# Attention and split convolution on one core: alternating the two kinds of attention blocks, and dividing by the row sums at the copy-out

## Chip, cores and metric

One core of a Trainium2 chip. The metric is the device time of one execution in microseconds. TensorE (PE) multiplies, VectorE (DVE) and ScalarE (ACT) work on tiles, GpSimd (POOL) too, and SyncE (SP) issues the DMAs.

## What is computed

Input x is 4 images of 256 channels and 64 x 64 pixels. The two layers, cut to what matters:

```python
# layer 0: attention over the 4096 pixels of an image
q, k, v = Wq @ xf, Wk @ xf, Wv @ xf                 # 32, 32 and 256 rows
attn = softmax((q.T @ k) / sqrt(32), axis=-1)       # 4096 x 4096
x = gamma * (Wo @ (v @ attn.T)) + x
# layer 1: in patches of 8 x 8
low = mean over 2 x 2;  high = p - upsample(low)
low = prelu(bn(mag_w @ low + mag_b))
high = prelu(bn(phase_w @ concat(high, roll(high, 1 row)) + phase_b))[:256]
out = upsample(low) + high
```

## The kernel before

**Tiling.** The queries of an image are worked on in 8 chunks of 512, so there are 32 chunks g. Values and output projection are one matrix, u. Each 32-bit number that needs it is a sum of two shorter ones (ph and pl, uh and ul), so a block is weighed with three products. The keys of an image are 32 tiles of 128. They come in two kinds, in 32 units t of a chunk:

- 16 *scored tiles* "d": TensorE multiplies keys with queries (`scores`, line 584, two tiles ahead), ScalarE takes two exponentials (`probabilities`, 754), VectorE forms the low part pl (`low_probabilities`, 1045), TensorE weighs: 12 matmuls into the four output banks O0 to O3 (`weigh_tile`, 621). Column 256 of uh is 1, so the sum of each row comes out as column C of the bank.
- 16 *kept blocks* "k": their scores were computed for the maxima one chunk earlier and kept in `saved` with queries on the partitions. ScalarE takes two exponentials (`slot_probabilities`, 763, at unit EXP_AT), VectorE the low part (`slot_low_probabilities`, 1049, at unit LOW_AT), SyncE transposes by DMA into a ring of four (`turn_slot`, 367), TensorE weighs 12 matmuls into one bank, k % 4 (`weigh_slot`, 636).

**Order.** It is written out by hand. UNITS (lines 53 to 56) is d0 to d5, then k0 d6 k1 d7 and so on to k9 d15, then k10 to k15. EXP_AT is 5 units ahead of a block's weighing, LOW_AT 3 (4 for the last ones). In between stand the other tasks of a chunk (lines 86 to 108), which use two banks M in turn: keys, queries and u of the next image ("kq", "u"; t = 0, 2), the output turned back ("y"; 5, 6), the two convolutions ("low" 20, 21; "high" 22, 24), 32 matmuls for the maxima of the next queries ("max", t = 3 to 28), and "negmax" (t = 30) with the queries' shift.

**Plans.** FULL is the plan of the first 24 chunks, LAST of the next 7, FINAL of the last: in the last image nothing is projected for a next one (no kq, u), and first scores are issued one unit before the chunk's end.

**The head of a chunk.** `copy_out` (748 on ScalarE for banks 0 and 2, 1028 on VectorE for 1 and 3) copies 257 columns of a bank when the last block of that bank, k12 to k15, is weighed. `normalise` (1033) on VectorE then takes the reciprocal of the sums, multiplies by the image's gain and scales the four copies. The first `weigh_tile` of the next chunk waits for the copies, the y tasks for `normalise`.

**SyncE's program of a FULL chunk**, each line waiting for its inputs, and everything behind it waiting too:

```python
sp.dma_start(xb, ...)                                   # 397
sp.wait_ge(qsave_ready, NCH + g + 1)                    # 398, the kq task, t = 0
sp.dma_start(flat(q_dram), qsave[96:128, :])            # 399
turn_slot(g, 0)
sp.wait_ge(qst_ready, g + 2); fetch_q(...)              # 403 to 406, low_q at t = 1
turn_slot(g, 1)
emptied(("u", 1)); store uh; store ul                   # 409 to 411, t = 2
sp.wait_ge(out_ready, g + 1); store z                   # 412 to 414
turn_slot(g, 2); turn_slot(g, 3); load xr; turn_slot(g, 4) ...
```

In LAST chunks lines 397 to 399 and 409 to 411 are left out, in FINAL 403 to 406 too. At an image's last chunk (`ends_image`) the loads of the next image's u stand between the `turn_slot` calls.

**The head of an image.** `find_scale` (903) on VectorE reduces the bound of x, GpSimd reduces it over the partitions (`reduce_bound`, 1187), and VectorE makes the scale of u from it. It runs in `before_image` (1134), ahead of the image's first chunk, and ScalarE waits for its result (`scaled`, line 842) ahead of that chunk.

Of the kernel before, what the change touches and what calls it, by code (L numbers as in the profile page):

```python
# [113 lines left out]
def attention_conv(nc, x, wqk, wv, wo, phase_w, mag_w, params, gamma, alpha, out, q_dram):  # L114
# [7 lines left out]
    with ctx:  # L122
# [27 lines left out]
        spare = sb("spare", [128, 10])  # L150
# [25 lines left out]
        oraw = sb("oraw", [128, SUB, UW])  # L176
# [26 lines left out]
        O = [ctx.enter_context(nc.psum_tensor(f"O{i}", [128, 512], f32)) for i in range(SUB)]  # L203
# [28 lines left out]
        u_direct_loaded, u_turned_loaded = sem("u_direct_loaded"), sem("u_turned_loaded")  # L232
        o02_out, o13_out, rs_step, on_ready = sem("o02_out"), sem("o13_out"), sem("rs_step"), sem("on_ready")
# [22 lines left out]
        def turns(eng, turn, before_image=None, before_last=None, image_end=None):  # L256


            inner = NCH - 1 if image_end else NCH
            with eng.Fori(0, B // 2 - 1) as pair_i:  # L260
                for parity in range(2):
                    if before_image:
                        before_image(pair_i * 2 + parity, parity)
                    with eng.Fori(0, inner) as c:
# [6 lines left out]
            with eng.Fori(0, inner) as c:  # L271
# [54 lines left out]
        def _(sp):  # L326
# [48 lines left out]
            def load_u(m, filled):  # L375

                sp.dma_start(uh_flat[:, m * SUB * UW:(m + 1) * SUB * UW], uh_dram[m]).then_inc(filled, 16)
                sp.dma_start(ul_flat[:, m * SUB * C:(m + 1) * SUB * C], ul_dram[m]).then_inc(filled, 16)

            def load_direct_u(g, m):  # L380

                sp.wait_ge(d_weighed, ND * g + SUB * (m + 1))
                load_u(m, u_direct_loaded)

            def load_turned_u(g, m):

                sp.wait_ge(k_weighed, NK * g + slot_of(SUB - 1, m) + 1 + RING)
                load_u(m, u_turned_loaded)

            def turn(g, parity, c, plan, scans, ends_image=False):  # L390
# [37 lines left out]
                turn_slot(g, 4)  # L428
                if ends_image:
                    load_direct_u(g, 1)  # L430
                turn_slot(g, 5)
# [4 lines left out]
                turn_slot(g, 8)  # L436
                if ends_image:
                    load_direct_u(g, 2)
                turn_slot(g, 9)
# [9 lines left out]
                if ends_image:  # L449
                    load_direct_u(g, 3)  # L450
                turn_slot(g, 14)
                turn_slot(g, 15)
                if ends_image:
                    load_turned_u(g, TURNED[2])
# [14 lines left out]
            sp.wait_ge(u_direct_loaded, 16 + 128 * (B - 1))  # L469
            sp.wait_ge(u_turned_loaded, 16 + 128 * (B - 1))  # L470
# [6 lines left out]
        def _(pe):  # L477
# [115 lines left out]
            def tasks(g, plan, keys_next, t):  # L593
                for n, task in plan.numbered.get(t, []):
# [6 lines left out]
                    elif kind == "y":  # L601
                        pe.wait_ge(on_ready, g + 2)
# [18 lines left out]
            def weigh_tile(g, i):  # L621

                if i == 0:
                    pe.wait_ge(u_direct_loaded, 128 * (g // NCH) + 16)
                pe.wait_ge(lo_ready, ND * g + i + 1)

                for j in range(SUB):
# [5 lines left out]
                    ins = nc.tensor.matmul(O[j][:, 0:UW], pl[:, i % 4, q], uh[:, i, :], start=False, stop=False)  # L633
# [47 lines left out]
            for n, task in TAIL.numbered[0]:  # L681
                pe.wait_ge(m_free[n % 2], use(TAIL, ALL, n))
                if task[0] == "y":
                    pe.wait_ge(on_ready, ALL + 2)
# [10 lines left out]
        def _(act):  # L695
# [52 lines left out]
            def copy_out(g, j):  # L748

                act.wait_ge(k_weighed, NK * g + RING - SUB + j + 1)  # L750
                act.wait_ge(high_ready, g + 1)
                nc.scalar.activation(oraw[:, j, :], O[j][:, 0:UW], ACT.Copy).then_inc(o02_out, 1)

            def probabilities(g, i):
                act.wait_ge(s_filled, ND * g + i + 1)
                if i >= 4:
                    act.wait_ge(d_weighed, ND * g + i - 3)
# [14 lines left out]
            def take(bank, task, g, parity, c):  # L772
# [6 lines left out]
                elif kind == "u":  # L779
                    act.wait_ge(u_stored, 32 * g + 32)  # L780
# [22 lines left out]
            def turn(g, parity, c, plan, scans):  # L803

                if plan is FULL:
# [52 lines left out]
        def _(dve):  # L858
# [10 lines left out]
            nc.vector.memset(half[:, :, :], -0.5).then_inc(on_ready, 1)  # L869
# [4 lines left out]
            nc.vector.memset(spare[:, 2:3], 0.0).then_inc(proj_free, 4)  # L874
            nc.vector.memset(spare[:, 3:4], 0.0).then_inc(k_weighed, RING)
            for i in range(RING):
                nc.vector.memset(spare[:, 6 + i:7 + i], 0.0).then_inc(turned[i], 16)
            nc.vector.memset(spare[:, 5:6], 0.0).then_inc(u_direct_loaded, 16)
            nc.vector.memset(spare[:, 4:5], 0.0).then_inc(u_turned_loaded, 16)
# [41 lines left out]
            dve.wait_ge(scanned0, NCH)  # L921
            find_scale(0, 0)
# [104 lines left out]

# [239 lines left out]
```

## Time and profile before

| | us |
|---|---|
| runs of the kernel before, median (lowest to highest) | 2342.92 (2342.83 to 2344.77) |
| the profiled execution, its own time | 2340.45 |
| its span | 2338.5 |
| TensorE busy, matmuls | 2205.9 (94%) |
| VectorE busy | 1782.4 (76%) |
| ScalarE busy | 1431.6 (61%) |
| GpSimd busy | 677.7 (29%) |
| mean granted clock of TensorE | 0.984 |

Busy times of matmuls have modelled ends, so TensorE's share isn't its share of peak. "Granted clock" is the part of the full 2.4 GHz that TensorE was given. A timeline row says what an instruction waited for in brackets: the idle time of its engine before it, and who released it. "SPq" is the queue in which SyncE issues. A line in the rows is a line of the kernel before.

### The profile page before, as it was taken

The numbers are of one execution on the slowest core, as the hardware profiler recorded it, in microseconds if no ns is written. First come the engines' busy times: TensorE is split into PE (matmuls) and PEld (weight loads), VectorE is DVE, ScalarE is ACT, GpSimd is POOL, SyncE is SP. The second block draws the span as 40 slices with busy tenths as digits, with TensorE's granted clock in tenths as the row PEclk, the third lists the DMA queues.
The fourth block names the chain that finished last, engine by engine and source line by source line (L and its number), as shares of the span: only waits on it lengthen the run. The fifth ranks groups of instructions, "written<-read, shape, count | busy, mean of one in ns | idle before, by whom it ended". The sixth has DMA issues, their size and how long they took to land.

```text
span 2338.5 us, 48099 instructions
## 1 busy us (share of the span) xinstructions
PE 2205.9 (94%) x16373; PEld 1764.1 (75%) x16373; DVE 1782.4 (76%) x3388; ACT 1431.6 (61%) x2547; POOL 677.7 (29%) x891
## 2 busy tenths in 40 slices
PE   5799999999989999999998999999999999999997
PEld 4577777777767777777777777777777777777776
DVE  6777877777867788877786877777877777778764
ACT  3457666657656666666656666566665656666663
POOL 3232332232322323322232321323322232233321
PEclk8799999999999999999999999999999999999998
DMA  4254444454554444444474443443445444344443
GB/s 159 59 115 94 99 109 102 84 117 99 135 131 85 110 107 92 109 108 97 93 168 102 99 99 72 104 96 91 103 111 133 75 89 93 77 82 88 84 86 64
DMA packets 596617, 235.02 MB, mean 101 GB/s; under 512 B 547072, under 2 KB 548352, under 8 KB 596576
## 3 DMA queue, kind: packets, MB, share of 16 engines
q1 hardware_dynamic: 596576, 234.51, 45.5%
q8 instruction: 22, 0.36, 0.1%
q14 instruction: 19, 0.16, 0.0%
HBM read 67.67 MB, written 32.53 MB: 43 GB/s over the span
## 4 chain that ended last, share of the span: by engine, by line
PE 64%; DVE 15%; issue 10%; DMA 5%; ACT 3%; POOL 1%; SPq 1%; DVEq 0%; ACTq 0%; POOLq 0%
PE M L482 13%; PE M L519 7%; PE O L631 7%; PE O L633 6%; PE O L632 6%; PE O L644 6%; PE O L646 6%; PE O L645 6%; DVE pq L1052 5%; DMA pt<-pq 4%; PE S L590 4%; DVE saved L947 4%; DVE pmax L943 2%; DVE pl L1047 2%; PE M L500 1%
## 5 line engine op out<-in xcount | busy, mean ns | idle before, releaser
L758 ACT ACTIVATE ph<-S 128x512 f16<-128x512 f32 x512 | 307.6, 601 | 525.5 <-PE S L590 524.8
L644 PE MATMUL O<-uh,pt 128*128 128x257 f16 x2048 | 568.2, 277 | 16.9 <-DMA pt<-pq 16.7
L631 PE MATMUL O<-uh,ph 128*128 128x257 f16 x2048 | 570.3, 278 | 4.5 <-DVE pl L1047 4.1
L633 PE MATMUL O<-uh,pl 128*128 128x257 f16 x2048 | 563.2, 275 | 0.0
L632 PE MATMUL O<-ul,ph 128*128 128x256 f16 x2048 | 561.8, 274 | 0.0
L646 PE MATMUL O<-uh,pt 128*128 128x257 f16 x2048 | 559.0, 273 | 0.0
L645 PE MATMUL O<-ul,pt 128*128 128x256 f16 x2048 | 555.7, 271 | 0.0
L947 DVE TENSOR_SCALAR_CACHE_REDUCE saved<-M 128x512 f32<-128x512 f32 x512 | 344.0, 687 | 257.0 <-PE M L519 253.0
L1047 DVE TENSOR_TENSOR pl<-p,ph 128x512 f16<-128x512 f32 x512 | 402.6, 787 | 60.5 <-ACT p L761 59.1
L519 PE MATMUL M<-kst,qst 96*128 (+1 forms) x1024 | 424.0, 442 | 20.9 <-DVE saved L947 16.2
L1052 DVE TENSOR_TENSOR pq<-saved,pq 128x512 f16<-128x512 f32 x512 | 387.6, 757 | 19.2 <-ACT saved L770 19.1
L943 DVE TENSOR_REDUCE pmax<-M 128x1 f32<-128x512 f32 (+1 forms) x512 | 341.4, 684 | 70.8 <-PE M L519 67.8
L769 ACT ACTIVATE pq<-saved,nbias 128x512 f16<-128x512 f32 x512 | 369.2, 721 | 1.3 <-DMA pt<-pq 1.3
L770 ACT ACTIVATE saved<-saved,nbias 128x512 f32<-128x512 f32 x512 | 367.9, 719 | 0.0
L761 ACT ACTIVATE p<-S 128x512 f32<-128x512 f32 x512 | 307.7, 601 | 0.0
L631 PEld LDWEIGHTS O<-uh,ph 128*128 128x128 f16 x2048 | 201.1, 98 | 133.7 <-issue 92.6
L644 PEld LDWEIGHTS O<-uh,pt 128*128 128x128 f16 x2048 | 198.8, 97 | 121.1 <-issue 52.4
L1215 POOL TENSOR_TENSOR zlow<-zlow,zlneg 128x256 f32<-128x256 f32 x32 | 23.8, 744 | 797.5 <-DVE zneg L1067 797.5
L590 PE MATMUL S<-qcur,kst 128*128 128x512 f32 x512 | 238.1, 475 | 16.5 <-ACT p L761 14.1
L519 PEld LDWEIGHTS M<-kst,qst 96*128 96x128 f32 x1024 | 188.3, 191 | 60.8 <-DVE saved L947 27.1
L633 PEld LDWEIGHTS O<-uh,pl 128*128 128x128 f16 x2048 | 201.7, 98 | 26.1
L646 PEld LDWEIGHTS O<-uh,pt 128*128 128x128 f16 x2048 | 197.8, 97 | 29.2
(161 smaller groups left out, 2907.4 us busy)
## 6 DMA issues: line engine op xcount, KB each, us to landing
xr<-in_x SPq DMA_DIRECT2D x53, 512.0 KB, 3.8
out_y<-z SPq DMA_DIRECT2D x33, 512.0 KB, 3.0
xb<-in_x SPq DMA_DIRECT2D x25, 512.0 KB, 3.7
pt<-pq SPq DMA_TRANSPOSE x512, 3.1
qraw<-q_scratch SPq DMA_DIRECT2D x99, 64.0 KB, 2.0
uh_scratch<-uh_next SPq DMA_DIRECT2D x24, 257.0 KB, 3.2
uh<-uh_scratch SPq DMA_DIRECT2D x24, 257.0 KB, 3.2
ul_scratch<-ul_next SPq DMA_DIRECT2D x24, 256.0 KB, 3.1
```

The source lines that it names most:

```text
L519: return nc.tensor.matmul(bank[:, :], qst[0:96, j * 128:(j + 1) * 128], kst[0:96, keys_at], start=True, stop=True)
L631: nc.tensor.matmul(O[j][:, 0:UW], ph[:, i % 4, q], uh[:, i, :], start=(i == 0), stop=False)
L632: nc.tensor.matmul(O[j][:, 0:C], ph[:, i % 4, q], ul[:, i, :], start=False, stop=False)
L633: ins = nc.tensor.matmul(O[j][:, 0:UW], pl[:, i % 4, q], uh[:, i, :], start=False, stop=False)
L644: nc.tensor.matmul(O[j][:, 0:UW], pt[:, k % RING, i, :], uh[:, t, :], start=False, stop=False)
L645: nc.tensor.matmul(O[j][:, 0:C], pt[:, k % RING, i, :], ul[:, t, :], start=False, stop=False)
L646: ins = nc.tensor.matmul(O[j][:, 0:UW], pt[:, k % RING, SUB + i, :], uh[:, t, :], start=False, stop=(ends and i == SUB - 1))
L769: nc.scalar.activation(pq[:, k % RING, 0, :], saved[:, k, :], ACT.Exp, scale=SCALE, bias=bias)
L943: nc.vector.tensor_reduce(pmax[:, j, ds(m, 1)], bank[:, :], AX.X, ALU.max).then_inc(free, 1)
L947: nc.vector.tensor_scalar(saved[:, slot_of(j, m), :], bank[:, :], 0.0, None, ALU.add, ALU.max, accum_out=pmax[:, j, m:m + 1]).then_inc(fre ...
L1047: nc.vector.tensor_tensor(pl[:, i % 4, :], p32[:, i % 2, :], ph[:, i % 4, :], ALU.subtract).then_inc(lo_ready, 1)
L1052: nc.vector.tensor_tensor(pq[:, k % RING, 1, :], saved[:, k, :], pq[:, k % RING, 0, :], ALU.subtract).then_inc(slot_low, 1)
```

## The change

Units now alternate from the first to the last: d0 k0 d1 k1 ... d15 k15. Exponentials of block k run at unit 2k - 4 (blocks 0 and 1 ahead of the chunk's own work), low parts at 2k - 2, at most 27. The four output banks are one tensor, O_all. Only k15 ends the chunk, so all banks are read after it: VectorE takes the reciprocal of the four sums from the banks themselves (`find_gains`), and both copies are made with that factor; `normalise` is gone. ScalarE's and VectorE's copies now wait for the gains. u has a semaphore for each eighth, and its loads move in SyncE's program. The scale is found inside the image's first chunk, after unit 0's low part, and ScalarE waits for it only at its first u task. Lines 397 to 415 of SyncE's program are as they were, apart from the u load taken out behind block 2.

```diff
-RISE = 6
-UNITS = [("d", i) for i in range(RISE)]
-for i in range(ND - RISE):
-    UNITS += [("k", i), ("d", RISE + i)]
-UNITS += [("k", k) for k in range(ND - RISE, NK)]
-AT = {unit: t for t, unit in enumerate(UNITS)}
-EXP_AT = [AT["k", k] - 5 for k in range(NK)]
-LOW_AT = [AT["k", k] - (3 if k < ND - RISE else 4) for k in range(NK)]
+UNITS = [unit for i in range(ND) for unit in (("d", i), ("k", i))]
+EXP_AT = [2 * k - 4 for k in range(NK)]
+LOW_AT = [min(2 * k - 2, MT - 5) for k in range(NK)]
...
             def load_direct_u(g, m):
 
-                sp.wait_ge(d_weighed, ND * g + SUB * (m + 1))
-                load_u(m, u_direct_loaded)
+                sp.wait_ge(d_weighed, ND * g + ND + SUB * (m + 1))
+                load_u(m)
...
                 turn_slot(g, 2)
-                if ends_image:
-                    sp.wait_ge(u_stored, 32 * g + 64)
-                    sp.sem_inc(turn_seen, 1)
-                    load_direct_u(g, 0)
                 turn_slot(g, 3)
...
             def weigh_slot(g, k):
 
-                if k == 0:
-                    pe.wait_ge(u_turned_loaded, 128 * (g // NCH) + 16)
+                if k % SUB == 0:
+                    pe.wait_ge(u_loaded[TURNED[k // SUB]], 32 * (g // NCH) + 16)
                 pe.wait_ge(turned[k % RING], 16 * (NK // RING * g + k // RING + 2))
-                j, ends = k % SUB, k >= NK - SUB
+                j, ends = k % SUB, k == NK - 1
...
             def copy_out(g, j):
 
-                act.wait_ge(k_weighed, NK * g + RING - SUB + j + 1)
+                act.wait_ge(rs_step, 2 * g + 2)
                 act.wait_ge(high_ready, g + 1)
-                nc.scalar.activation(oraw[:, j, :], O[j][:, 0:UW], ACT.Copy).then_inc(o02_out, 1)
+                nc.scalar.activation(oraw[:, j, :], O[j][:, 0:C], ACT.Copy, scale=rs[:, j:j + 1]).then_inc(o02_out, 1)
...
                 elif kind == "u":
+                    if task[1] == 0:
+                        act.wait_ge(scaled, g // NCH + 2)
                     act.wait_ge(u_stored, 32 * g + 32)
...
             def turn(g, parity, c, plan, scans):
 
+                for k in range(NK):
+                    if EXP_AT[k] < 0:
+                        slot_probabilities(g, k)
                 if plan is FULL:
                     copy_out(g, 0)
                 probabilities(g, 0)
...
-            def before_image(image, parity):
-                act.wait_ge(scaled, image + 2)
-
-            turns(act, turn, before_image)
+            turns(act, turn)
...
+            def find_gains(g):
+
+                dve.wait_ge(k_weighed, NK * g + RING)
+                dve.wait_ge(o02_out, 2 * g)
+                nc.vector.reciprocal(rs[:, :], O_all[:, :, C]).then_inc(rs_step, 1)
+                dve.wait_ge(rs_step, 2 * g + 1)
+                gain = ogain[:, ds((g + (ALL - 1)) % ALL // NCH, 1)]
+                nc.vector.tensor_tensor(rs[:, :], rs[:, :], gain.to_broadcast([128, SUB]), ALU.mult).then_inc(rs_step, 1)
+
             def copy_out(g, j):
...
                 dve.wait_ge(rs_step, 2 * g + 2)
-                for j in range(SUB):
-                    ins = nc.vector.tensor_scalar(oraw[:, j, 0:C], oraw[:, j, 0:C], rs[:, j:j + 1], None, ALU.mult)
-                ins.then_inc(on_ready, 1)
+                nc.vector.tensor_scalar(oraw[:, j, :], O[j][:, 0:C], rs[:, j:j + 1], None, ALU.mult).then_inc(o13_out, 1)
...
-            def turn(g, parity, c, plan, scans):
+            def turn(g, parity, c, plan, scans, scale_of=None):
+                for k in range(NK):
+                    if LOW_AT[k] < 0:
+                        slot_low_probabilities(g, k)
                 if plan is not FULL:
                     low_probabilities(g, 0)
+                find_gains(g)
                 copy_out(g, 1)
                 copy_out(g, 3)
...
-                    if t == (0 if plan is FULL else 1):
-                        normalise(g)
+                    if t == 0 and scale_of is not None:
+                        find_scale(scale_of + 1, 1 - parity)
```

## Rows read from the trace of the kernel before

**Rows 1.** The page, part 4: share of the chain that ended last, by engine

```profile
PE 64%; DVE 15%; issue 10%; DMA 5%; ACT 3%; POOL 1%; SPq 1%; DVEq 0%; ACTq 0%; POOLq 0%
```

**Rows 2.** The chain in order of time (start us, us, what), longest pieces, two successive chunks

```profile
431.39 3.06 PE M L482 x12
...
501.13 3.06 PE M L482 x12
```

**Rows 3.** The chain in order of time, a chunk's end and the next one's head

```profile
453.45 0.47 PE S L590 x2
453.93 2.80 PE M L482 x18
...
456.97 0.12 PE O L631
```

**Rows 4.** The waits of SyncE's queue: waiter, releaser: us in total, times, longest us

```profile
SPq L399 <- ACT qraw L778: 183.9, 24, 20.6
```

**Rows 5.** Timeline of VectorE: start, us, instruction, count, idle before and its releaser

```profile
453.49 0.42 DVE L1031 COPY oraw<-O 128x257 f32<-128x257 f32 x1 [0.71 <-PE O L646]
...
456.71 0.17 DVE L1036 RECIPROCAL rs<-oraw 128x4 f32<-128x4 f32 x1
457.14 0.16 DVE L1039 TENSOR_TENSOR rs<-rs,ogain 128x4 f32<-128x4 f32 x1 [0.25 <-DVE rs L1036]
...
670.25 0.15 DVE L915 RECIPROCAL uscale<-prod 128x1 f32<-128x1 f32 x1
...
1991.51 0.69 DVE L1047 TENSOR_TENSOR pl<-p,ph 128x512 f16<-128x512 f32 x1 [2.51 <-ACT p L761]
```

**Rows 6.** Timeline of ScalarE: block 2's exponentials, and the head of an image

```profile
460.19 0.73 ACT L769 ACTIVATE pq<-saved,nbias 128x512 f16<-128x512 f32 x1
...
461.42 0.60 ACT L758 ACTIVATE ph<-S 128x512 f16<-128x512 f32 x1
...
670.68 0.39 ACT L752 ACTIVATE oraw<-O 128x257 f32<-128x257 f32 x1 [17.34 <-DVE uscale L915]
```

**Rows 7.** Timeline of SyncE's queue (issues), the head of a chunk and of an image

```profile
467.43 1.27 SPq L344 DMA_DIRECT2D qraw<-q_scratch  x3
469.31 1.24 SPq L372 DMA_TRANSPOSE pt<-pq  x1
470.83 0.39 SPq L410 DMA_DIRECT2D uh_scratch<-uh_next  x1
...
473.13 1.35 SPq L372 DMA_TRANSPOSE pt<-pq  x1
...
674.55 0.35 SPq L399 DMA_DIRECT2D q_scratch<-qraw  x1
```

**Rows 8.** One tile, pt, as SyncE's queue loads it, all 512 transposes

```profile
DMA to landing us min/median/max: 3.0/3.1/5.3
```

**Rows 9.** Timeline of TensorE: four instructions that waited

```profile
476.81 0.28 PE L644 MATMUL O<-uh,pt 128*128 128x257 f16 x1 [0.55 <-DMA pt<-pq]
...
519.92 0.29 PE L525 MATMUL M<-ident,nmax 128*128 128x128 f32 x1 [0.35 <-DVE nmax L954]
...
672.09 0.79 PE L590 MATMUL S<-qcur,kst 128*128 128x512 f32 x1 [5.78 <-ACT p L761]
...
1992.44 0.28 PE L631 MATMUL O<-uh,ph 128*128 128x257 f16 x1 [0.28 <-DVE pl L1047]
```

**Rows 10.** Windows: busy us (instructions) of each engine, granted TensorE clock, DMA share, GB/s

```profile
122.00:127.00 5.00, 2.47 (x19) 1.71 (x17) 4.42 (x6) 3.25 (x5) 4.26 (x6) 1.00 1.14 198
127.00:132.00 5.00, 4.86 (x26) 3.52 (x27) 2.37 (x4) 2.30 (x4) 1.79 (x3) 0.66 0.40 121
665.00:670.00 5.00, 1.32 (x12) 1.11 (x10) 0.34 (x3) 0.00 (x0) 0.38 (x1) 1.00 0.49 170
...
674.00:676.00 2.00, 2.00 (x11) 1.25 (x8) 1.68 (x8) 1.97 (x5) 0.00 (x0) 0.50 0.17 41
```

**Rows 11.** The waits, over the whole span: TensorE's weight loads behind the normalised low part

```profile
PEld M L482 <- ACT zlow L788: 18.6, 24, 0.8
```

More of the change, by code:

```diff
@@ L201, in attention_conv @@
         odd_hi, odd_lo = [buf[:, :, 1:ROWS + 1, :].rearrange("p t r w -> p t (r w)") for buf in (hh, hl)]
-        O = [ctx.enter_context(nc.psum_tensor(f"O{i}", [128, 512], f32)) for i in range(SUB)]
+        O_all = ctx.enter_context(nc.psum_tensor("O", [128, SUB, 512], f32))
+        O = [O_all[:, j, :] for j in range(SUB)]
         S = [ctx.enter_context(nc.psum_tensor(f"S{i}", [128, 512], f32)) for i in range(2)]
@@ L231, in attention_conv @@
         u_stored = sem("u_stored")
-        u_direct_loaded, u_turned_loaded = sem("u_direct_loaded"), sem("u_turned_loaded")
-        o02_out, o13_out, rs_step, on_ready = sem("o02_out"), sem("o13_out"), sem("rs_step"), sem("on_ready")
+        u_loaded = [sem(f"u_loaded{m}") for m in range(NCH)]
+        o02_out, o13_out, rs_step = sem("o02_out"), sem("o13_out"), sem("rs_step")
         pairs_ready, low_ready, high_ready = sem("pairs_ready"), sem("low_ready"), sem("high_ready")
@@ L263, in turns @@
                         before_image(pair_i * 2 + parity, parity)
-                    with eng.Fori(0, inner) as c:
+                    if image_start:
+                        image_start(pair_i * 2 + parity, pair_i * (2 * NCH) + parity * NCH, parity, scans=True)
+                    with eng.Fori(begin, inner) as c:
                         turn(pair_i * (2 * NCH) + parity * NCH + c, parity, c, FULL, scans=True)
@@ L270, in turns @@
                 before_image(B - 2, 0)
-            with eng.Fori(0, inner) as c:
+            if image_start:
+                image_start(B - 2, (B - 2) * NCH, 0, scans=False)
+            with eng.Fori(begin, inner) as c:
                 turn((B - 2) * NCH + c, 0, c, FULL, scans=False)
@@ L428, in turn @@
                 turn_slot(g, 4)
+                turn_slot(g, 5)
                 if ends_image:
[L430 to L431 removed]
+                    load_direct_u(g, 0)
                 turn_slot(g, 6)
@@ L449, in turn @@
                 if ends_image:
-                    load_direct_u(g, 3)
+                    load_direct_u(g, 2)
                 turn_slot(g, 14)
+                if ends_image:
+                    load_turned_u(g, TURNED[2])
                 turn_slot(g, 15)
                 if ends_image:
-                    load_turned_u(g, TURNED[2])
+                    load_direct_u(g, 3)
+                    sp.wait_ge(u_stored, 32 * g + 64)
+                    sp.sem_inc(turn_seen, 1)
                     load_turned_u(g, TURNED[3])
@@ L468, in _ @@
             sp.wait_ge(u_stored, 32 * (1 + ALL - NCH))
-            sp.wait_ge(u_direct_loaded, 16 + 128 * (B - 1))
-            sp.wait_ge(u_turned_loaded, 16 + 128 * (B - 1))
+            for m in range(NCH):
+                sp.wait_ge(u_loaded[m], 16 + 32 * (B - 1))
             sp.wait_ge(xr_loaded, 16 * (1 + ALL))
@@ L632, in weigh_tile @@
                     nc.tensor.matmul(O[j][:, 0:C], ph[:, i % 4, q], ul[:, i, :], start=False, stop=False)
-                    ins = nc.tensor.matmul(O[j][:, 0:UW], pl[:, i % 4, q], uh[:, i, :], start=False, stop=False)
+                    ins = nc.tensor.matmul(O[j][:, 0:UW], pl[:, i % 4, q], uh[:, i, :],
+                                           start=False, stop=(i == ND - 1 and j < SUB - 1))
                 ins.then_inc(d_weighed, 1)
             def weigh_slot(g, k):
-                if k == 0:
-                    pe.wait_ge(u_turned_loaded, 128 * (g // NCH) + 16)
+                if k % SUB == 0:
+                    pe.wait_ge(u_loaded[TURNED[k // SUB]], 32 * (g // NCH) + 16)
                 pe.wait_ge(turned[k % RING], 16 * (NK // RING * g + k // RING + 2))
-                j, ends = k % SUB, k >= NK - SUB
+                j, ends = k % SUB, k == NK - 1
                 for i in range(SUB):
@@ L865, in done @@
                 dve.wait_ge(dstep, chain[0])
-            nc.vector.memset(half[:, :, :], -0.5).then_inc(on_ready, 1)
+            nc.vector.memset(half[:, :, :], -0.5)
             nc.vector.memset(quarter[:, :], 0.25).then_inc(out_stored, 16)
@@ L877, in _ @@
                 nc.vector.memset(spare[:, 6 + i:7 + i], 0.0).then_inc(turned[i], 16)
-            nc.vector.memset(spare[:, 5:6], 0.0).then_inc(u_direct_loaded, 16)
-            nc.vector.memset(spare[:, 4:5], 0.0).then_inc(u_turned_loaded, 16)
+            for m in range(NCH):
+                nc.vector.memset(spare[:, 10 + m:11 + m], 0.0).then_inc(u_loaded[m], 16)
             dve.wait_ge(consts, 1)
@@ L921, in _ @@
             dve.wait_ge(scanned0, NCH)
+            bound_x(0)
             find_scale(0, 0)
@@ L1136, in before_image @@
                 dve.wait_ge(xs_scanned, image * NCH + 1)
-                find_scale(image + 1, 1 - parity)
-            turns(dve, turn, before_image)
+                bound_x(1 - parity)
+            turns(dve, turn, before_image,
+                  image_start=lambda image, g, parity, scans: turn(g, parity, 0, FULL, scans, scale_of=image))
+            find_gains(ALL)
             copy_out(ALL, 1)
             copy_out(ALL, 3)
-            normalise(ALL)
             for n, task in TAIL.numbered[0][:CT]:
```

45 lines of the change are left out of this document (20 added, 25 removed).

## The prediction

> **What bounds the kernel now.** I read first the chain that ended last: it runs through TensorE for 64% of the span [rows 1]. TensorE is the resource to watch, and it has little room: two successive chunks lie 501.13 - 431.39 = 69.74 us apart [rows 2]. So I read, in one steady chunk (it ends at about 453.45 and the next one begins there), what each engine does at the head of a chunk, where the change moves most. Call T the moment at which the last weighing of the old chunk ends: T = 453.45 [rows 3]. After T TensorE runs two score tiles, the 18 projection matmuls (key/query block and first u half) in 2.80 us, a third score tile, and starts weighing d0 at 456.97, T + 3.5 [rows 3]. That cover is what hides the copy-out now. The third thing to read is SyncE's queue, which issues everything in program order: at every FULL chunk it stands at line 399, the store of the new queries, waiting for ScalarE's copy, 183.9 us in 24 waits [rows 4]. Today nobody pays for that, because the first transposed block k0 is weighed only in unit 6.
>
> **The change, part by part.**
>
> *Order of units.* Now six d come first and six k last; after it is d0, k0, d1, k1 and so on. The matmuls are the same ones, so their busy time moves by nothing. What moves is when k0, k1, k2 are wanted: unit 1, 3, 5 instead of 6, 8, 10. SyncE's program at the head is not changed: in a FULL chunk it loads xb, waits for the saved queries, stores them (line 399), and only then issues the transpose of k0; then it waits for qst, fetches three query blocks, and transposes k1; then it waits for u1, stores uh and ul, waits for and stores z, and transposes k2. Each of these is now in front of a block that TensorE wants at once.
>
> *When k0 lands (24 FULL chunks).* The banks are now read only when all k are weighed. VectorE can start 0.04 us after T (its copy of a bank did, 453.49 against 453.45) [rows 3, 5]; reciprocal to multiply is 457.14 - 456.71 = 0.43, the multiply 0.16 [rows 5]: gains at T + 0.63. ScalarE starts 670.68 - 670.40 = 0.28 after a VectorE result [rows 5, 6]: first bank copied from T + 0.91. From there to the store of the queries is 674.55 - 670.68 = 3.87 (copy, two exponentials, copy, two exponentials, keys, queries) [rows 6, 7]. New on that way is the pair of exponentials for block 2, which now runs at t = 0 ahead of the projection's copies: 461.42 - 460.19 = 1.23 [rows 6]. Store of queries at T + 0.91 + 3.87 + 1.23 = T + 6.0. The next issue of SyncE is some 0.7 later (473.13 - 470.83 = 2.30 for three) [rows 7], and a transpose lands in 3.1 us by the median, or 476.81 - 473.13 = 3.7 as seen by TensorE in this chunk [rows 7 to 9]. k0 is there at T + 9.8 to T + 10.4. TensorE is ready for it at T + 3.5 + 1.25 = T + 4.75 (12 matmuls at 0.11 apart is 1.25 to 1.3). **Wait for k0: 5.0 to 5.6 us, I take 5.3.** The same wait stands ahead of everything later on TensorE, since it runs in order. The matmuls of d0 don't wait for the gains: ScalarE's second copy is done by T + 2.6 and the low part of d0 (one exponential pair from T + 1.2, then 0.69) by T + 3.1 [rows 5, 6], before T + 3.5. So for FULL chunks the copy-out itself costs nothing; the cover is the projections.
>
> *Clock after that wait.* In the stretch 665 to 670 TensorE is busy 1.32 of 5 us, and in 674 to 676 the granted clock is 0.50, the lower level of 1.2 GHz; after a shorter gap (2.47 of 5 us busy in 122 to 127) the next 5 us were granted 0.66 on the mean [rows 10]. Each costs time: half of some 5 us in the first case, 0.34 x 5 = 1.7 in the second. For a wait of 5.3 I take 2.6. The Trainium skill (TensorE: Matmul & The Clock Gate, section "HAM oscillation — how this bites in real kernels") describes the same thing for a kernel that waits on a DMA in every tile; this trace agrees, with 0.50 after its longest gap [rows 10]. The same page (section "What's actually happening") would put the ramp below 1% of a typical span, which here would be under 23 us in all instead of the some 100 us that my rows give; by it the sum would be near 2578.
>
> *k1 and k2 in FULL chunks.* k1 needs qst: ScalarE's u copy, the exponentials of d2, the query copy, then VectorE; about T + 9.5, then the fetch, 469.31 - 467.43 = 1.88 [rows 7], issue at T + 11.5, landed T + 14.6 to 15.2. TensorE, at k0 until T + 11.5 to 12.8, then score, u1 (1.4) and d1, wants it at T + 14.7 or later: no cost. k2 needs u1: from the end of u1's matmuls, ScalarE 0 to 0.8 (it is at block 3's exponentials) + 0.7, VectorE 0.85, SyncE 0.15 + 2.30 for uh, ul and z [rows 7], landing 3.1 to 3.7: 7.1 to 8.5. TensorE has d1, k1, d2 (1.25 each), two scored maxima, a score tile and the y transposes between, some 5.4. **Wait for k2: 1.7 to 3.1, I take 2.2**, with 0.8 of clock (less than the second case of [rows 10], whose gap was longer).
>
> *End of a FULL chunk.* d15 is now second to last, so its low part (0.69, pitch 0.60) stands on VectorE between the last maximum and d15, behind nbias, while TensorE has only the negative maxima to do; they already wait 0.35 us there [rows 9]. One more low part (d14) stands before the last maximum. I take +0.9 (0 to 1.2). The wait of the high convolution for zlow, 18.6 us in 24 [rows 11], loses ScalarE work ahead of it (no exponentials at odd t): -0.4 of 0.8. Sum for a FULL chunk: 5.3 + 2.6 + 2.2 + 0.8 + 0.9 - 0.4 = 11.4; 24 x 11.4 = 274.
>
> *LAST chunks (7) and FINAL.* There are no projections, so nothing covers the copy-out: VectorE comes to the gains after d0's low part, T' + 0.5 (T' the end of the old chunk here), ScalarE's first copy ends 0.43 + 0.16 + 0.28 + 0.39 later, weighing starts at 1.9 after T' instead of 0.75 (1992.44, where it now waits for that low part) [rows 5, 9]: +1.15. k0's transpose is at once. k1's is behind the query fetch, which waits for qst: ScalarE does d1's exponentials, block 2's 1.23, d2's exponentials, the query copy (0.63); VectorE 0.68; the fetch 1.88; landing 3.1 to 3.7 [rows 5 to 9]: T' + 11.6 to 12.2. TensorE wants k1 at T' + 6.3, and the maximum before it waits for qst too (it waits 0.4 now): +5.2. Clock 2.6. Together 8.95; 7 x 8.95 + 1.15 for FINAL = 64.
>
> *Scale of the next image.* The wait for GpSimd's reduction leaves ScalarE's head of the chunk; now it holds TensorE 5.78 us at 672.09 [rows 9] and the clock is low after it (2.5) [rows 10]; three image starts, the first one shorter, are some 23 us. After the change VectorE waits for it behind d0's low part until T + 7.5, still before k0 lands, so all 23 are saved: -23. What is late next there is k0, as in every chunk, which is in the 274.
>
> *At nothing.* Four scalings of 0.29 leave VectorE and the two copies there become scaled copies of the same size; VectorE isn't late there. The u loads move in SyncE's queue, each behind units that are weighed by then; if that cover were gone, a load of two issues (1.5 us) would be ahead of one transpose, in 3 chunks only.
>
> **Sum.** 2340.45 (profiled execution: span 2338.5 and 2 us around it) + 274 + 64 - 23 = 2655. The median of the runs, 2342.92, is 2.5 above the profiled one, inside my rounding. I predict 2655.
>
> **Rivals.** (a) *The stalls come, the clock does not fall*: 24 x 3.4 + 7 x 2.6 = 100 less, 2555. For it: the wait of 0.55 at 476.81 [rows 9] is followed by no slow stretch. Against: [rows 10], where both longer gaps are. (b) *Only k0 stalls*: the k2 chain is met by slack that the k0 wait gives, since ScalarE and VectorE run ahead meanwhile: 24 x 3.0 less, 2583. (c) *Landings are slow*: the transposes behind plain DMAs land at their maximum, 5.3 [rows 8], for k0 and k2: 2 x 1.9 more, the clock 0.7, and k4 waits 1 behind the y units: 24 x 5.5 more, 2787. (d) *Not slower*: the blocks are early. The mechanism: alternation evens out what VectorE and ScalarE owe TensorE, the 2 to 3.5 us of waits inside a chunk shrink by 1, and the image starts give 23: 2340 - 32 - 23 = 2285. It decides only if the head costs less than about 1.7 us a chunk, which asks that k0 land by T + 6.5, before the queries are even stored at T + 6.0 plus a landing. Only an issue order other than the program's could do it.
>
> **How the numbers follow.** Main 0.58, (a) 0.12, (b) 0.13, (c) 0.12, (d) 0.04, and 0.01 for no change. The short ends of all terms (k0 5.0, k2 1.7, no clock, end 0) give 2340 + 24 x 6.3 + 46 - 23 = 2514; the long ones (5.6, clock 3, 3.1 with 1.6, end 1.2, zlow nothing) 2340 + 24 x 14.5 + 68 - 23 = 2733, and (c) lies beyond. Range 2530 to 2740. 0.2% is about what a measurement can tell from no change: faster 0.04, same 0.01, slower 0.95.
>
> **What would show it.** In the changed profile: TensorE's weighing of k waits for the transposes some 5 us at unit 1 of each FULL chunk (with k2 in all about 24 x 7.5 = 180 us) and at k1 in LAST chunks; SyncE's wait at the query store stays, the first transpose follows it within 1 us; granted clock is 0.5 for some us after it; the chunk distance is 81 instead of 69.7, and some 9 more than now in the last image. If k0's transpose is issued before the query store, my main step is wrong; if the distance is under 71, so is the whole.

## The result

The changed kernel takes 2649.88 us (median of 4 runs, 2644.64 to 2654.14) against 2342.88 for the kernel before: a ratio of 1.1309, 95% interval 1.1283 to 1.1334. The forecast was 2655, its range 2530 to 2740. The profiled execution has a span of 2652.3 against 2338.5, so 313.8 us more.

The page of the changed kernel, busy times of part 1 and shares of part 4; the line of [rows 1] answers to the second:

```profile
PE 2291.6 (86%) x16373; PEld 1806.2 (68%) x16373; DVE 1733.9 (65%) x3263; ACT 1449.2 (55%) x2547; POOL 741.6 (28%) x891
...
PE 51%; DVE 16%; DMA 12%; issue 9%; ACT 9%; SPq 3%; DVEq 1%; ACTq 0%; POOL 0%; POOLq 0%
```

TensorE's matmuls are as many, but they take 86 us more of modelled busy time, and TensorE's share of the last chain falls from 64% to 51% while DMA's rises from 5% to 12%. The mean granted clock fell from 0.984 to 0.954.

The chain in order of time shows the distance of two chunks; the first two lines are the transposes of k2 in two successive FULL chunks, the others those of k1 in two LAST chunks:

```profile
521.89 3.77 DMA pt<-pq
...
603.99 3.78 DMA pt<-pq
...
2203.86 3.06 DMA pt<-pq
...
2278.09 3.06 DMA pt<-pq
```

These FULL chunks are 603.99 - 521.89 = 82.10 apart instead of 69.74 [rows 2], LAST chunks 74.23. Not every FULL chunk is as long: by the ends of their weighings they lie 79.9 to 82.2 apart.

The head of one FULL chunk, as SyncE's queue issued it. To compare with [rows 7]:

```profile
508.90 0.37 SPq L399 DMA_DIRECT2D q_scratch<-qraw  x1
509.49 1.26 SPq L372 DMA_TRANSPOSE pt<-pq  x1
512.59 1.27 SPq L344 DMA_DIRECT2D qraw<-q_scratch  x3
514.06 1.23 SPq L372 DMA_TRANSPOSE pt<-pq  x1
519.68 0.39 SPq L410 DMA_DIRECT2D uh_scratch<-uh_next  x1
...
521.29 0.39 SPq L414 DMA_DIRECT2D out_y<-z  x1
521.89 3.00 SPq L372 DMA_TRANSPOSE pt<-pq  x2
```

The last weighing of the old chunk ends at 502.88 here (call it T again; its line is the first of the next lines). The queries are stored at 508.90, T + 6.0; k0's transpose follows at T + 6.6, the query fetch waits until 512.59 and k1 follows it, the stores of u wait until 519.68 and k2 follows them and z. What TensorE, ScalarE and VectorE did in the same stretch:

```profile
502.60 0.27 PE L648 MATMUL O<-uh,pt 128*128 128x257 f16 x1
```

```profile
503.01 0.18 DVE L1042 RECIPROCAL rs<-O 128x4 f32<-128x4 f32 x1 [0.68 <-PE O L648]
```

```profile
503.65 0.47 ACT L755 ACTIVATE oraw<-O,rs 128x256 f32<-128x256 f32 x1 [1.55 <-DVE rs L1045]
...
506.28 0.76 ACT L772 ACTIVATE pq<-saved,nbias 128x512 f16<-128x512 f32 x1
...
508.13 0.59 ACT L781 ACTIVATE qraw<-M 32x512 f32<-32x512 f32 x1
```

```profile
500.05 0.28 PE L632 MATMUL O<-uh,ph 128*128 128x257 f16 x1 [0.56 <-DVE pl L1054]
...
512.62 0.40 PE L646 MATMUL O<-uh,pt 128*128 128x257 f16 x1 [4.90 <-DMA pt<-pq]
...
525.71 0.28 PE L646 MATMUL O<-uh,pt 128*128 128x257 f16 x1 [2.79 <-DMA pt<-pq]
...
535.43 0.28 PE L646 MATMUL O<-uh,pt 128*128 128x257 f16 x1 [0.74 <-DMA pt<-pq]
...
2206.96 0.40 PE L646 MATMUL O<-uh,pt 128*128 128x257 f16 x1 [4.27 <-DMA pt<-pq]
```

VectorE takes the sums 0.13 after T, ScalarE copies from T + 0.77, and the exponentials of block 2 (506.28) are ahead of the keys (507.50) and the queries (508.13). TensorE waits 0.56 us for the low part of d15 before T, then 4.90 us for k0, 2.79 for k2, 0.74 for k4, and in a LAST chunk 4.27 for k1. All waits of this kind:

```profile
PE O L646 <- DMA pt<-pq: 229.0, 91, 5.0
```

```profile
SPq L399 <- ACT qraw L781: 229.6, 24, 15.4
```

Matmuls waited 229.0 us for transposed blocks, where the kernel before has 16.7. SyncE's wait at the query store is there as before (229.6 us in 24, [rows 4] had 183.9), but now it stands in front of something wanted.

Windows of the changed kernel, columns as in [rows 10]: after the wait for k0, after the wait for k2, and after the wait for k1 in a LAST chunk. After each the granted clock (third column from the right) is at or near 0.5. Taken over the 4 us from the first matmul behind a wait, it is low behind k0 in all 24 FULL chunks and behind k2 in 17 of them:

```profile
512.00:514.00 2.00, 1.38 (x7) 0.99 (x8) 0.27 (x1) 0.00 (x0) 0.00 (x0) 0.58 0.12 35
514.00:516.00 2.00, 2.00 (x11) 1.58 (x10) 0.00 (x0) 0.16 (x1) 0.00 (x0) 0.57 0.62 142
...
527.00:529.00 2.00, 2.00 (x10) 1.57 (x9) 0.00 (x0) 0.20 (x1) 0.00 (x0) 0.50 0.00 0
...
2207.00:2209.00 2.00, 2.00 (x10) 1.41 (x11) 0.00 (x0) 0.00 (x0) 0.00 (x0) 0.50 1.06 279
```

### The profile page after: what moved, and what is told of

The parts are those of the page before. It is cut to its first block, busy times and chain, and to the rows that moved or that the text cites. A ratio compares the mean times of both kernels' runs of the same rounds, so it can differ in the third digit from the quotient of the medians.

```text
span 2652.3 us, 48023 instructions
## 1 busy us (share of the span) xinstructions
PE 2291.6 (86%) x16373; PEld 1806.2 (68%) x16373; DVE 1733.9 (65%) x3263; ACT 1449.2 (55%) x2547; POOL 741.6 (28%) x891
## 4 chain that ended last, share of the span: by engine, by line
PE 51%; DVE 16%; DMA 12%; issue 9%; ACT 9%; SPq 3%; DVEq 1%; ACTq 0%; POOL 0%; POOLq 0%
DMA pt<-pq 11%; PE M L482 8%; PE O L646 7%; PE O L648 6%; PE O L647 6%; PE M L519 6%; PE O L632 4%; PE O L634 4%; PE O L633 4%; DVE pq L1059 4%; DVE saved L957 3%; PE S L590 3%; DVE pl L1054 3%; ACT saved L773 2%; ACT p L764 2%
## 5 line engine op out<-in xcount | busy, mean ns | idle before, releaser
L646 PE MATMUL O<-uh,pt 128*128 128x257 f16 x2048 | 591.2, 289 | 231.6 <-DMA pt<-pq 229.0
L648 PE MATMUL O<-uh,pt 128*128 128x257 f16 x2048 | 585.4, 286 | 0.0
L647 PE MATMUL O<-ul,pt 128*128 128x256 f16 x2048 | 580.9, 284 | 0.0
L519 PE MATMUL M<-kst,qst 96*128 (+1 forms) x1024 | 429.5, 446 | 25.2 <-DVE saved L957 14.7
L646 PEld LDWEIGHTS O<-uh,pt 128*128 128x128 f16 x2048 | 205.4, 100 | 359.1 <-DMA pt<-pq 266.1
L1054 DVE TENSOR_TENSOR pl<-p,ph 128x512 f16<-128x512 f32 x512 | 408.5, 798 | 28.0 <-ACT p L764 28.0
L1059 DVE TENSOR_TENSOR pq<-saved,pq 128x512 f16<-128x512 f32 x512 | 374.6, 732 | 28.6 <-ACT saved L773 27.3
L296 POOL TENSOR_TENSOR zneg<-y 128x256 f32<-128x256 f32 x64 | 49.4, 794 | 767.7 <-DVE y L1066 767.7
L590 PE MATMUL S<-qcur,kst 128*128 128x512 f32 x512 | 248.9, 496 | 3.3 <-DVE qcur L975 2.4
L1227 POOL TENSOR_TENSOR zlow<-zlow,zlneg 128x256 f32<-128x256 f32 x32 | 35.5, 1110 | 743.1 <-DVE zneg L1074 743.1
L648 PEld LDWEIGHTS O<-uh,pt 128*128 128x128 f16 x2048 | 206.6, 101 | 37.1
```

Of the source, the lines that this page charges most:

```text
L519: return nc.tensor.matmul(bank[:, :], qst[0:96, j * 128:(j + 1) * 128], kst[0:96, keys_at], start=True, stop=True)
L646: nc.tensor.matmul(O[j][:, 0:UW], pt[:, k % RING, i, :], uh[:, t, :], start=False, stop=False)
L647: nc.tensor.matmul(O[j][:, 0:C], pt[:, k % RING, i, :], ul[:, t, :], start=False, stop=False)
L648: ins = nc.tensor.matmul(O[j][:, 0:UW], pt[:, k % RING, SUB + i, :], uh[:, t, :], start=False, stop=(ends and i == SUB - 1))
L1054: nc.vector.tensor_tensor(pl[:, i % 4, :], p32[:, i % 2, :], ph[:, i % 4, :], ALU.subtract).then_inc(lo_ready, 1)
L1059: nc.vector.tensor_tensor(pq[:, k % RING, 1, :], saved[:, k, :], pq[:, k % RING, 0, :], ALU.subtract).then_inc(slot_low, 1)
```

## Experiments

Every ratio is to the kernel before, run beside it on the same chip (medians 2339.83 to 2340.67). The changed kernel was not run again beside them, and the kernel before took 2342.88 beside it, so a difference to its 2649.88 carries some 3 us.

### k0's transpose ahead of the query store

```diff
 # SyncE, FULL chunk
+turn_slot(g, 0)
 sp.wait_ge(qsave_ready, NCH + g + 1)
 sp.dma_start(flat(q_dram), qsave[96:128, :])
-turn_slot(g, 0)
```

> The changed kernel with one edit in SyncE's program of a FULL chunk: the transpose of k0 is issued ahead of the wait for the saved queries. Theory (the blocks wait for the issue order of SyncE): the wait for k0 is gone, but k1 is still behind the query fetch and lands at about T + 14.7, where TensorE now wants it at T + 9.4: one wait of some 5 us with 1.5 us of low clock at k1. u1 is projected 5 us earlier, so uh and ul are stored before k2's turn and the k2 wait (2.8, and its clock 1.6) is gone. So 24 x 4.4 = 105 us less: 2545 us (2520 to 2575). LAST chunks unchanged. Rival 1 (k0 is late because its exponentials, its low part or the transpose itself are late at a chunk's head, not for the order of issue): k0's wait stays near 5 us, 2650. Rival 2 (the two waits are independent prices): 24 x 6.6 less with k1 at no cost, 2490.

Measured: 2581.08, ratio 1.103 (1.101 to 1.105). The wait for k0 is gone: in the chunk of the lines below d0 ends at 569.84 and k0 starts there. The wait stands at k1 instead, behind the query fetch:

```profile
574.88 1.27 SPq L344 DMA_DIRECT2D qraw<-q_scratch  x3
576.35 1.24 SPq L372 DMA_TRANSPOSE pt<-pq  x1
```

```profile
569.84 0.27 PE L647 MATMUL O<-uh,pt 128*128 128x257 f16 x1
...
579.45 0.40 PE L647 MATMUL O<-uh,pt 128*128 128x257 f16 x1 [3.80 <-DMA pt<-pq]
```

k1's transpose is issued at 576.35, 1.47 behind the fetch, and TensorE waits 3.80 for it; k2 (585.90) doesn't wait. So rival 1 falls, and the move of the wait came as the theory said. The size did not: 69 us were saved, not 105, and the time lies above the forecast range and far above the 2490 of rival 2. In the profile k1's wait is followed by 12 matmuls in 2.40 and again in 2.38 us, so the slow stretch is as long as behind the longer wait, and u1 and d1 now wait 0.36 and 0.30 us for VectorE.

### Exponentials of block 2 behind the projection's copies

```diff
 # ScalarE, t = 0
-slot_probabilities(g, 2)
 take(kq); take(u 0)
+slot_probabilities(g, 2)
 probabilities(g, LEAD)
```

> The changed kernel with the two exponentials of block 2 behind the projection's copies at t = 0 instead of ahead of them. The output is the same. Theory (k0's landing is one chain: gains, copies, exponentials, query copy, query store, transpose): the query store is 1.23 us earlier after T, so k0's wait is 4.9 - 1.2 = 3.7 in the FULL chunks, and the end moves by 24 x 1.2 = 30, with up to 10 of clock: 2615 (2600 to 2625). k2 unchanged. Rival (another chain holds k0, its own low part on VectorE or the xb load in the queue): no change, 2650.

Measured: 2596.55, ratio 1.1096 (1.1076 to 1.1116), 53 us less than the changed kernel and a little under the forecast range. TensorE's wait for k0, and the windows after it:

```profile
576.75 0.28 PE L646 MATMUL O<-uh,pt 128*128 128x257 f16 x1 [3.65 <-DMA pt<-pq]
```

```profile
578.00:580.00 2.00, 2.00 (x19) 1.89 (x17) 0.00 (x0) 1.49 (x3) 0.00 (x0) 1.00 0.38 100
588.00:590.00 2.00, 1.64 (x8) 1.19 (x9) 0.00 (x0) 0.00 (x0) 0.00 (x0) 0.60 0.51 93
```

The wait is 3.65, 1.25 shorter, as the chain says (the block's exponentials have a pitch of 1.23 [rows 6]). In 24 chunks that is some 29 of the 53 us. The rest goes with the clock. In this chunk it stays at 1.00 after this wait, where it was 0.58 after the one of 4.90, and behind the wait for k2, 2.51 us, it falls to 0.60 all the same. But this chunk is an exception. In the FULL chunk ahead of it the wait for k0 is as long, and the clock is low behind it:

```profile
497.86 0.40 PE L646 MATMUL O<-uh,pt 128*128 128x257 f16 x1 [3.67 <-DMA pt<-pq]
```

```profile
498.00:500.00 2.00, 2.00 (x11) 1.37 (x10) 0.10 (x1) 0.00 (x0) 0.00 (x0) 0.50 0.18 48
```

Taken over the 4 us behind each wait, the clock is low behind k0 in 20 of the 24 FULL chunks and behind k2 in 6, against 24 and 17 in the changed kernel. Of the 23 waits for k0 of 3.39 to 3.72 us, 20 had low clock behind them and 3 had none.

### Filling the wait for k0

```diff
 # TensorE, FULL chunk, ahead of the wait for k0's transpose
+for _ in range(60):
+    nc.tensor.matmul(O[0][:, 384:512], uh[:, 0, 0:128], uh[:, 0, 0:128], start=False, stop=False)
 pe.wait_ge(turned[0], ...)
```

> The changed kernel with 60 extra matmuls of 128 columns (3.4 us at 0.056) ahead of the wait for k0 in FULL chunks; they write columns of the first output bank that nothing reads, so the output is the same. They fit in the wait of 4.9 us. Theory (the slow stretch after k0 is the clock's answer to the idle time): k0's 12 matmuls take 1.25 us again instead of 2.4, and the 1.5 us of slow work after the wait go: 24 x 1.5 = 36 less, 2614 (2605 to 2625). The wait before k0 shrinks to about 1.3, k2's stays. Rival (the slow stretch comes from something else, such as the transposes landing or the load on the memory): no gain, 2650.

Measured: 2613.73, ratio 1.1177 (1.116 to 1.1194): 36.2 us less with 1440 matmuls more.

```profile
494.54 3.51 PE L644 MATMUL O<-uh 128*128 128x128 f16 x60
499.64 0.28 PE L649 MATMUL O<-uh,pt 128*128 128x257 f16 x1 [1.58 <-DMA pt<-pq]
```

```profile
500.00:502.00 2.00, 2.00 (x19) 1.85 (x17) 0.00 (x0) 0.59 (x2) 0.00 (x0) 1.00 0.34 98
```

The 60 matmuls take 3.51, TensorE then waits 1.58 more, so k0 comes 499.64 - 494.54 = 5.10 after the moment at which TensorE could have taken it. In the changed kernel it is 5.06 (the last matmul of d0 starts at 507.45 and the next could follow 0.11 later), so the block is as late as there. The granted clock after it is 1.00, in 23 of the 24 FULL chunks. So the slow stretch is the answer to idle time. Rival (a) of the prediction, that the clock does not fall, is out.

Not all of the 36.2 us need be k0's. The wait for k2 is as long as before, but behind it the clock is now low in 10 of the 24 FULL chunks instead of 17. One of the others:

```profile
432.11 0.28 PE L649 MATMUL O<-uh,pt 128*128 128x257 f16 x1 [2.77 <-DMA pt<-pq]
```

```profile
434.00:436.00 2.00, 2.00 (x18) 1.55 (x17) 1.69 (x3) 2.00 (x4) 0.92 (x2) 1.00 0.00 0
```

In the changed kernel a wait of 2.79 had 0.50 behind it. What k0 costs is read from the timeline of the changed kernel: the 12 matmuls behind the wait take 2.41 instead of 1.25, the groups from there to d1 0.36 longer, so 1.5 us a chunk. The runs of both kernels spread by some 5 us around their medians, so the total does not tell the two places apart.

### Blocks 0 to 3 ahead of what stood before them

```diff
-LOW_AT = [min(2 * k - 2, MT - 5) for k in range(NK)]
+LOW_AT = [-2, -1] + [min(2 * k - 2, MT - 5) for k in range(2, NK)]
 # SyncE:  xb, k0, k1, query store, k2, query fetch, k3, uh, ul, z, xr, k4
 # was:    xb, query store, k0, query fetch, k1, uh, ul, z, k2, k3, xr, k4
```

> The changed kernel with the transposes of k0 and k1 ahead of the query store, k2 ahead of the query fetch, k3 ahead of the stores of uh, ul and z, and the low part of block 1 at the chunk's head. Theory: the waits for k0, k1 and k2 and the low clock behind them go, in FULL chunks 11 us each (4.9 + 1.5, 2.8 + 1.6, with some 0.5 left at k2), in LAST chunks 4.3 + 0.4 + 2.3 each: 2650 - 24 x 10.6 - 7 x 7 = 2347, range 2320 to 2370, so about the kernel before. Rival (alternation itself costs: VectorE or ScalarE can't keep up when d and k alternate from the start, or the copy-out at the end of the chunk costs): TensorE then waits for low parts, exponentials or the copied banks in their place, 2450 or more.

Measured: 2471.36, ratio 1.0566 (1.0549 to 1.0582). This took back 178.5 of the 307 us, not 303, a clear miss, and the rival's threshold of 2450 is passed. k0 and k1 don't wait any more outside the images' first chunks. What is left at the head of a chunk is u1 behind VectorE's part of the keys (0.53), d2 behind its low part (0.62), and a block that did not wait before:

```profile
562.99 0.39 SPq L413 DMA_DIRECT2D uh_scratch<-uh_next  x1
...
564.45 0.39 SPq L417 DMA_DIRECT2D out_y<-z  x1
565.16 0.40 SPq L422 DMA_DIRECT2D xr<-in_x  x1
565.76 1.51 SPq L372 DMA_TRANSPOSE pt<-pq  x1
```

```profile
570.80 0.28 PE L647 MATMUL O<-uh,pt 128*128 128x257 f16 x1 [2.03 <-DMA pt<-pq]
```

SyncE issues uh, ul, z and xr from 562.99 to 565.16 and k4's transpose at 565.76; TensorE has it at 570.80, 5.04 later, after a wait of 2.03. The clock falls behind this wait in 5 of the 24 FULL chunks. The longest landing of this kernel's transposes, 8.1 us, is that of k0 in the second image's first chunk, right behind two pairs of u loads and xb; in the kernel before the median is 3.1 and the longest 5.3 [rows 8].

### k4 ahead of z and xr, and then the exponentials too

```diff
 # SyncE: ..., k3, uh, ul,
-z, xr, k4
+k4, z, xr
```

> The kernel with the blocks ahead of the stores (2471), and now the transpose of k4 also ahead of the store of z and the load of xr. In the earlier kernel k4's transpose was issued 0.2 us after its low part was done and still landed 5 us later, right behind 1.5 MB of plain transfers (uh, ul, z, xr), and TensorE waited 1.9 us for it in each FULL chunk and had 1.3 of low clock. Theory (a transpose lands late because of the plain transfers issued just ahead of it): with two of the four behind it, it lands 1 to 2 us earlier, the wait falls to 0.7 or less and the clock stays: 24 x 2 to 3 less, 2410 (2395 to 2430), unless k5, which now has z and xr ahead of it, takes over 1 us of the wait. Rival (k4 lands late because two transposes follow each other in the queue): no change, 2471.

Measured: 2445.34, ratio 1.0446 (1.0429 to 1.0464), 26 us less, above the forecast range of 2395 to 2430. k4 doesn't wait any more, and k5, which now follows z and xr, does:

```profile
558.88 1.25 SPq L372 DMA_TRANSPOSE pt<-pq  x1
560.62 0.39 SPq L418 DMA_DIRECT2D out_y<-z  x1
561.34 0.40 SPq L423 DMA_DIRECT2D xr<-in_x  x1
561.93 5.27 SPq L372 DMA_TRANSPOSE pt<-pq  x2
```

```profile
567.04 0.28 PE L647 MATMUL O<-uh,pt 128*128 128x257 f16 x1 [1.27 <-DMA pt<-pq]
```

The time from issue to landing of these two transposes, k4 (558.88) and k5 (561.93):

```profile
DMA to landing us min/median/max: 3.1/3.1/3.1
DMA to landing us min/median/max: 5.1/5.1/5.1
```

So the theory stands in its weaker form, the one with k5: the wait of 1.9 to 2.0 has become one of 1.27 at the next block, and the clock no longer falls behind it, but for the first chunk. The landings say more than the theory did. k4, with uh and ul issued 2.7 and 2.1 us ahead of it, lands in 3.1; k5, with z and xr 1.3 and 0.6 ahead, takes as long as k4 did with all four. So it was z and xr that made k4 late. The rival, two transposes in a row, is out: k0 and k1 of this kernel follow each other directly and land in 3.2 (medians of the FULL chunks).

> The kernel of the run before (blocks 0 to 4 ahead of the stores), and the exponentials of block 2 behind the projection's copies. Theory (what is left at a chunk's head is ScalarE's order: u1 waits 0.5 and d2's low part 0.6 us behind those exponentials): both waits go, 24 x 1.0 less than the run beside it, unless block 2's transpose, whose low part is now later, takes it back. Rival (TensorE waits for VectorE's order, not ScalarE's): no change against the run beside it. Neither is expected to be under the kernel before, 2341, since the waits of 0.9 us at a chunk's end and 0.9 at the low convolution stay.

The edit is that of the exponentials of block 2 above, on this kernel. Measured: 2447.90, ratio 1.046 (1.0442 to 1.0477), no change against the run beside it. In its profile the wait of u1 for VectorE is gone, but the one for d2's low part is still 0.62, and the matmul for a maximum ahead of d2 waits 0.71 instead of 0.16 for VectorE, whose u part now comes later:

```profile
553.90 0.49 PE L520 MATMUL M<-kst,qst 96*128 x1 [0.71 <-DVE ul_next L1088]
...
555.01 0.28 PE L633 MATMUL O<-uh,ph 128*128 128x257 f16 x1 [0.62 <-DVE pl L1056]
```

So what is left at the head is not ScalarE's order alone. How much is left can be read from the run before this one: its FULL chunks lie 73.8 apart, 4.2 more than in the kernel before. TensorE's waits of over 0.1 us come to 4.7 a chunk there and to 1.8 in the kernel before, which is 2.9 of the 4.2. The largest are k5 (1.27 in the chunk shown), d2 (0.61), d15 (0.56), u1 (0.49) and k2 (0.45). The other 1.3 are matmuls that follow each other more slowly with no wait that the profile shows; no run tested what holds them.

### The order alone undone

```diff
-UNITS = [unit for i in range(ND) for unit in (("d", i), ("k", i))]
-EXP_AT = [2 * k - 4 for k in range(NK)]
-LOW_AT = [min(2 * k - 2, MT - 5) for k in range(NK)]
+# UNITS, EXP_AT and LOW_AT of the kernel before (its lines 52 to 59)
```

> The changed kernel with one part undone: the order of units and the times of exponentials and low parts are those of the kernel before (six d first, six k last). The copy-out divided by the sums, the scale inside the chunk and the u loads by eighths stay. Theory (the whole loss is the order): near the kernel before; the scale gives some 15 us, the late copy-out costs nothing in FULL chunks, where the projections cover it, and 1.15 us in each of the 8 others: 2341 - 15 + 9 = 2335 (2327 to 2345). Rival (the copy-out after the last block costs some of the loss in every chunk): 1 us or more in each of 32, 2358 or more.

Measured: 2353.94, ratio 1.0055 (1.0041 to 1.0069), between theory and rival. The order is therefore worth 2649.9 - 2353.9 = 296 us. The rest of the change isn't free. In the last image the first matmul of d0 now waits for ScalarE's copy, which it didn't before:

```profile
L637 PE MATMUL O<-uh,ph 128*128 128x257 f16 x2048 | 567.4, 277 | 14.5 <-ACT oraw L760 10.4 <-DVE pl L1059 1.6
```

The eight waits for the copied banks, 10.4 us, are those of the last image's eight chunks (LAST and FINAL). In FULL chunks, most distances are 70.3 to 70.5 us against 69.6: by the starts of the units, d1 takes 0.33 longer, the stretches with the maxima at t = 4 and 5 0.33 and 0.35, and 0.4 of it is given back at k2. That is 24 x 0.75 = 18 us; the last image's chunks, 1.2 longer each, make up the rest of the 29 below.

### The scale alone

```diff
 # ScalarE and VectorE of the kernel before
-before_image: bound of x, wait for GpSimd, scale, all ahead of the image's first chunk
+before_image: bound of x; find_scale after unit 0's low part; ScalarE waits at its first u task
```

> The kernel before with one part of the change alone: the scale of the next image is found after unit 0's low part inside an image's first chunk, and ScalarE waits for it at its first u task. Theory: the waits of 5.8 us at two image starts and of 3.1 at the first, with the low clock behind them (2.5 each), become a wait of about 1.8 for u1 and d2: 15 to 20 us less, 2325 (2320 to 2330); the 23 us that the prediction gave to this part are the bound that holds only where k0 is late anyway. Rival (the wait is the same, only in another place, since everything behind it on VectorE waits too): within 0.2% of the kernel before, 2343.

Measured: 2325.57, ratio 0.9936 (0.9922 to 0.995). In this kernel one chunk, written out by hand at an image's start, takes the last image's gain, so its output differs from the reference's; the next kernel takes the gain by the image and is otherwise the same.

> The kernel before with the scale of the next image found inside the image's first chunk, as in the run of that part alone, here with the gain taken by the index of the image in every chunk (in the earlier kernel the chunk after an image's start that is written out by hand took the last image's gain, at the same cost). Same time as that run: ratio 0.994, 2326 (2322 to 2330). Rival (that the wait only moves): within 0.2% of the kernel before.

Measured: 2324.99, ratio 0.9936 (0.9922 to 0.9949). TensorE's wait at the image start:

```profile
665.34 0.51 PE L594 MATMUL S<-qcur,kst 128*128 128x512 f32 x1 [2.84 <-ACT p L765]
```

It is 2.84 instead of 5.78 [rows 9], and the work after it goes at full pace. That is 15.7 us for three image starts, 0.6% and clear of noise; this kernel is faster than the one before and the changed one. From one run to the next the parts are 2341 - 15.7 (scale) + 29 (copy-out and u loads, 2353.9 against 2325.0) + 296 (order) = 2650. Being steps of one chain they must meet the total; each price holds with the parts ahead of it in place.

## Why the prediction was right, point by point

**Where k0 is late.** Right, nearly to the tenth: gains, copies, two pairs of exponentials, block 2's pair, keys, queries, store at T + 6.0 as forecast and as measured; transpose at T + 6.7 forecast, 6.6 measured; wait 5.3 forecast, 4.90 measured. The run with block 2's exponentials moved shows that it is this chain, and the one with k0's transpose moved shows that it is the order of issue.

**Clock.** The mechanism was right, the sizes off in both directions: 2.6 forecast behind k0, 1.5 measured; 0.8 forecast behind k2, about 1.6 in the chunk shown (12 matmuls in 2.19 instead of 1.25, and the four groups behind them 0.7 longer), but only in 17 of 24 chunks, so some 1.1 in the mean. The step that failed is that the price was taken to grow with the length of the wait. A drop cost 1.5 to 1.6 behind either wait; what differed was whether there was one: behind the waits for k0 of 4.6 to 5.0 always, behind those of 3.39 to 3.72 in 20 of 23 chunks, behind k2's of 2.3 to 2.8 in some chunks and not in others, and less often when the wait ahead of it was filled. The Trainium skill (TensorE: Matmul & The Clock Gate, "What's actually happening") puts the ramp below 1% of a typical kernel span. Here the clock falls again in every chunk, and behind k0 alone that is 24 x 1.5 = 36 of 2650 us, 1.4%.

**k2.** Forecast 2.2, measured 2.79, inside the given 1.7 to 3.1. Its chain is the forecast one (u1, uh, ul, z, then the transpose).

**End of a FULL chunk.** d15 waits 0.56 for its low part, and the end takes 14.15 - 12.97 - 0.31 (a score tile that moved there) = 0.87 longer, as forecast (0.9).

**Low convolution.** Forecast -0.4, measured about 0: matmuls and weight loads still wait for zlow. The term is the one that failed. The row that answers to [rows 11]:

```profile
PEld M L482 <- ACT zlow L793: 20.9, 24, 0.9
```

In the kernel before the same wait is 18.6 us, so it hasn't shrunk. Even units now carry the exponentials of d and of k, which may be what ScalarE is late with at the low tile; no run tested that.

**Sum of a FULL chunk.** 4.9 + 1.5 + 2.8 + 1.6 + 0.9 + 0 = 11.7, forecast 11.4; the distance in the steady chunk grew by 12.4. Of the other 0.7, k4's wait is 0.74, since its transpose, issued 1.1 behind the load of xr, lands in 3.8 and not in 3.1; k2 already waited 0.55 in the kernel before [rows 9], so 0.5 are not taken apart. That the total came within 0.2% is partly luck: the terms missed by -0.4 (k0), -1.1 (its clock), +0.6 (k2), +0.8 (its clock), +0.4 (low convolution) and +0.74 (k4, taken at nothing), and a lower price for k0 met higher ones elsewhere.

**LAST chunks.** Forecast +8.95; the distance is 74.2 against 65.7, +8.5. k1 waits 4.27 behind the query fetch, forecast 5.2, and d0 1.23 for the copied banks, where it waited 0.28 for its low part before, so 0.95 more, forecast 1.15. FINAL is off: 60.35 against 55.94, +4.4, where 1.15 was forecast; k3's transpose is waited for there, 1.56 us, which the prediction did not have.

**"At nothing" was not nothing.** The copy-out at the end costs 0.75 us a FULL chunk when the order is the old one, by the heads of d1 and the first maxima, not by d0, where I had looked. In the changed kernel d1 and these maxima come behind the wait for k0 and show no such wait; no run changed the order without the copy-out. The 23 us for the scale are right only beside the same wait; alone the part gives 15.7, since TensorE then still waits 2.84 us.

**Rivals.** (a) is excluded by the filled wait. (b) that k2 finds slack: it waits. (c) slow landings: not at the 5.3 that it took (k0 3.1 after its issue, k2 3.8), but k4 does wait 0.74 for a landing of 3.8, and with the blocks moved ahead a landing of 5.0 is the largest wait left. (d) would have needed another order of issue, and even with it the best kernel with alternating units is 1.0446.

## What to carry to other kernels

When work is reordered on the engine that sets the time, write down the program of the queue that feeds it, and for each block which waits stand in front of its transfer: a queue that issues in order hands its longest wait to everything behind it, and moving one block ahead only passes the wait to the next. Price a wait on TensorE with the clock behind it, counted over all chunks and not in one, and ask what the new wait hides: here it stood ahead of a cost of 0.75 us a chunk and made a gain of 15.7 look like 23. Of a change with several parts, measure the parts: one of them was worth keeping, at a ratio of 0.9936.

## What was not expected of the hardware

The length of a wait alone did not decide whether the granted clock fell. Behind waits of 3.39 to 3.72 us it fell in 20 chunks and not in 3 of the same run. Behind the wait for k2 of about 2.8 us it was 0.50 in the changed kernel and 1.00, in the chunk shown, where the wait ahead of it had been filled with matmuls.

A DMA transpose landed in 3.1 us by the median. With z and xr (512 KB each) issued 1.3 and 0.6 us ahead of it, it took 5.1; with uh and ul (257 and 256 KB) 2.7 and 2.1 us ahead, it took 3.1; with uh, ul and z in the 2.2 us ahead, 3.8.
